# State-space layers of a hybrid network on one core: a new order of the work on TensorE, VectorE, ScalarE and GpSimd, and z in another PSUM bank

## The reference, cut to what matters

```
for i in range(6):
    residual = hidden if residual is None else hidden + residual
    h = rmsnorm(residual, norm_w[i])
    u, z = split(h @ in_w)                      # 64 -> 2 x 128
    uc = silu(causal_conv4(u) + cb)
    dt_r, Bm, Cm = split(uc @ xp_w)             # 16, 16, 16
    dt = softplus(dt_r @ dt_w + dt_b)
    # per channel d and state s, over the 256 positions:
    #   state = exp(dt * A) * state + dt * uc * Bm ;  y = sum_s state * Cm
    y = scan(uc, dt, -exp(A_log), Bm, Cm) + uc * D
    hidden = (y * silu(z)) @ out_w
```

## Time and profile before

| | us |
|---|---|
| median of 3 timed runs (lowest, highest) | 526.92 (526.82, 527.38) |
| the profiled execution | 528.41 |
| its span in the trace | 526.6 |
| TensorE busy (weight loads) | 376.8, 72% (255.9, 49%) |
| VectorE busy | 335.8, 64% |
| ScalarE busy | 256.5, 49% |
| GpSimd busy | 220.5, 42% |
| mean granted clock of TensorE | 0.826 of 2.4 GHz |

### The profile page before, as it was taken

One profiled execution on the slowest core, in us unless ns is written; L12 is line 12 of the kernel. 1 busy time (PEld: TensorE's weight loads), 2 busy tenths in 40 slices (PEclk: granted clock), 3 DMA queues, 4 the chain that ended last, 5 costly groups with the idle time before them and its releaser, 6 DMA issues.

```text
span 526.6 us, 5516 instructions
## 1 busy us (share of the span) xinstructions
PE 376.8 (72%) x1634; PEld 255.9 (49%) x1634; DVE 335.8 (64%) x577; ACT 256.5 (49%) x679; POOL 220.5 (42%) x218
## 2 busy tenths in 40 slices
PE   5753799769995894557878568587856878786563
PEld 3542566446664532235556345455644555564442
DVE  3984665445553432277777877777777777778773
ACT  1300366436561633565556565555656555565132
POOL 0760690000000002286657667665766666577000
PEclk9975899979996796557878897977889678787967
DMA  7500000000000000324051341405134150413000
GB/s 278 224 1 1 0 2 0 1 1 1 1 1 0 0 1 0 86 76 162 1 165 60 130 135 58 161 1 164 60 128 156 37 162 1 160 34 128 0 1 11
DMA packets 10424, 34.11 MB, mean 65 GB/s; under 512 B 2272, under 2 KB 2592, under 8 KB 10272
## 3 DMA queue, kind: packets, MB, share of 16 engines
q1 hardware_dynamic: 10400, 33.83, 18.8%
HBM read 33.49 MB, written 0.33 MB: 64 GB/s over the span
## 4 chain that ended last, share of the span: by engine, by line
PE 43%; DVE 21%; ACT 11%; issue 10%; POOL 9%; DMA 5%; POOLq 0%; SPq 0%; DVEq 0%; ACTq 0%
PE PS L521 11%; POOL big L1278 5%; DMA big<-spill 3%; PE PS L356 3%; PE PS L405 3%; PE PS L413 3%; PE PS L366 3%; PE PS L344 3%; DVE dt L862 2%; PE PS L263 2%; DVE big L880 2%; PE PS L498 2%; DVE big L890 2%; ACT sg L1080 1%; PE PS L490 1%
## 5 line engine op out<-in xcount | busy, mean ns | idle before, releaser
L521 PE MATMUL PS<-big,cst 128*128 128x256 f32 x384 | 119.9, 468 | 37.6 <-DVE big L890 37.6
L880 DVE TENSOR_TENSOR_SCAN big<-PS,big 128x1024 f32<-128x1024 f32 x48 | 109.7, 2286 | 35.7 <-POOL big L1278 35.7
L1278 POOL TENSOR_TENSOR big<-dtu,big 128x1024 f32<-128x1024 f32 x48 | 113.7, 2394 | 39.7 <-DVE dtu L869 36.0
L521 PEld LDWEIGHTS PS<-big,cst 128*128 128x128 f32 x384 | 87.2, 236 | 57.1 <-DVE big L890 42.4
L1112 ACT ACTIVATE PS<-dt,amat 128x255 f32<-128x255 f32 x192 | 78.9, 459 | 19.8 <-DVE dt L866 13.0
L890 DVE TENSOR_TENSOR big<-big,PS 128x1024 f32<-128x1024 f32 x48 | 58.4, 1216 | 3.5 <-PE PS L508 3.0
L977 ACT ACTIVATE big<-PS 128x512 f32<-128x512 f32 (+1 forms) x49 | 29.1, 596 | 51.9 <-PE PS L344 28.2
L1219 POOL TENSOR_TENSOR hbias<-wmt,half_t 128x1 f32<-128x1 f32 x6 | 1.2, 194 | 124.6 <-PE PS L476 124.6
L508 PE MATMUL PS<-stack,pick_b 96*128 96x256 bf16 x192 | 34.4, 309 | 11.7 <-DVE big L890 9.6
L733 DVE TENSOR_REDUCE big<-PS 128x2 f32<-128x512 f32 x32 | 22.1, 691 | 28.0 <-PE PS L405 15.3
L1014 ACT ACTIVATE big<-PS,big 128x256 f32<-128x256 f32 x64 | 29.6, 472 | 13.0 <-DVE big L733 13.0
(11 more groups left out here) (253 smaller groups left out, 676.4 us busy)
## 6 DMA issues: line engine op xcount, KB each, us to landing
big<-spill SPq DMA_DIRECT2D x48, 512.0 KB, 5.8
wmt<-in_wm SPq DMA_DIRECT2D x6, 418.0 KB, 3.3
w3t<-in_w SPq DMA_DIRECT2D x1, 1588.0 KB, 13.1
w2t<-in_w SPq DMA_DIRECT2D x1, 896.0 KB, 9.9
cst<-in_const SPq DMA_DIRECT2D x1, 848.0 KB, 7.6
w5t<-in_w SPq DMA_DIRECT2D x1, 812.0 KB, 14.9
w0t<-in_w SPq DMA_DIRECT2D x1, 416.5 KB, 3.8
w1t<-in_w SPq DMA_DIRECT2D x1, 385.0 KB, 8.1
```

Of the source, the lines that this page charges most:

```text
L521: last = pe.matmul(yps, ident, hc[:, g, s], start=False, stop=(g == NSG - 1 and s == SG - 1), skip_group_check=True)
L880: v.tensor_tensor_scan(flat(hst[g % 2][:]), flat(da[g % 2]), flat(dbu[:, g]), 0.0, ALU.mult, ALU.add).then_inc(sem("m_h"), 1)
L1278: pool.tensor_tensor(dbu[:, g], dtu[b][:].unsqueeze(1).to_broadcast([P, SG, N]), bsp[b][:, SG * g:SG * (g + 1)], ALU.mult).then_inc(sem("m ...
```

## The change

Nothing is computed differently; the same instructions are issued in another order, with other waits, and z is written to another bank. In a step u the orders are now:
- VectorE: polynomial/dt/dtu(u), gate(u-1), residual(u-1), scan 0, C product 0, scan 1, C product 1, uc(u+1), scan 2, C product 2, scan 3, C product 3.
- TensorE: sums 3 of u-1, out projection(u-1), C spread 0, skip product, transposes(u+1), C spread 1, in-projection(u+1), sums 0, x-projection(u+1), C spread 2, dt projection(u+1), sums 1, C spread 3, sums 2.
- ScalarE: decay 0, norm, decay 1, layer weights, ht, decay 2, Tanh part, first half of decay 3, xd, second half of decay 3, softplus.
- GpSimd: product 1, scale, (layer weights), product 2, product 3, (rates), gz and stack, product 0 of u+1.

`zps` is moved to bank 7, beside `ups`. The first Tanh waits for the z matmul, and uc waits for ScalarE's copy of z (`m_zs`).

```diff
-        yps, zps = PS[:, 6, 0:N], PS[:, 6, N:2 * N]
+        yps = PS[:, 6, 0:N]
-        tr, dtp = PS[:, 7, N:2 * N], PS[:, 7, N:2 * N]
+        tr, zps, dtp = (PS[:, 7, N:2 * N] for _ in range(3))
...
-                pe.matmul(ups, wcv[k][:, P:2 * P], ht[b][:, 1:1 + N], start=False, stop=True).then_inc(sem("m_up"), 1)
-                pe.matmul(zps, WM.of(wmt[k], "inz", 64), ht[b][0:64, 3:3 + N], start=opens, stop=True,
-                          skip_group_check=True).then_inc(sem("m_zp"), 1)
+                pe.matmul(ups, wcv[k][:, P:2 * P], ht[b][:, 1:1 + N], start=False, stop=True)
+                pe.matmul(zps, WM.of(wmt[k], "inz", 64), ht[b][0:64, 3:3 + N], start=True, stop=True)\
+                    .then_inc(sem("m_zp"), 1)
...
                 pe.wait_ge(sem("m_stack"), u + 1)
-                spread_c(u, b, 0)
                 if not first:
                     out_proj(u + -1, pk, nb)
+                spread_c(u, b, 0)
                 sum_skip(u, k, b)
+                if not last:
+                    prep_transpose(u + 1, nk, nb)
                 pe.wait_ge(sem("m_hc"), u * NSG + 1)
                 spread_c(u, b, 1)
                 if not last:
-                    prep_transpose(u + 1, nk, nb)
+                    prep_in(u + 1, nk, nb, i * 2 + (s + 1) // 2 + 1)
                 sum_y(u, b, 0)
                 if not last:
-                    prep_in(u + 1, nk, nb, i * 2 + (s + 1) // 2 + 1)
+                    prep_x(u + 1, nk, nb)
                 pe.wait_ge(sem("m_hc"), u * NSG + 2)
                 spread_c(u, b, 2)
                 if not last:
-                    prep_x(u + 1, nk, nb)
+                    prep_dt(u + 1, nk, nb)
                 sum_y(u, b, 1)
-                if not last:
-                    prep_dt(u + 1, nk, nb)
...
                 v.wait_ge(sem("m_sig"), u * 2 + 1)
+                v.wait_ge(sem("m_zs"), u + 1)
...
+                prep_dt(u, b)
+                if not first:
+                    gate(u + -1, pk, nb)
+                if not first:
+                    residual(u + -1, nb)
                 for g in range(NSG):
...
-                    if g == 0 and not first:
-                        gate(u + -1, pk, nb)
-                    if g == 2 and not last:
-                        prep_uc(u + 1, nk, nb)
-                    if g == 3 and not last:
-                        prep_dt(u + 1, nb)
...
-                    if g == 0 and not first:
-                        residual(u + -1, nb)
+                    if g == 1 and not last:
+                        prep_uc(u + 1, nk, nb)
...
-                decay(u, k, b, 0, not first)
-                decay(u, k, b, 1, not first)
+                decay(u, k, b, 0, behind=not first)
...
                     prep_norm(u + 1, nk, nb, ("ln_norm", 6 * NG) if first else None)
+                decay(u, k, b, 1, behind=not first)
+                if not last:
                     prep_weights(u + 1, nk, nb)
+                    prep_ht(u + 1, nk, nb)
                 decay(u, k, b, 2)
                 if not last:
-                    prep_ht(u + 1, nk, nb)
-                decay(u, k, b, 3)
+                    prep_sig(u + 1, nk, nb)
+                decay(u, k, b, 3, range(2))
                 if not last:
-                    prep_sig(u + 1, nk, nb)
                     prep_xd(u + 1, nk, nb)
+                decay(u, k, b, 3, range(2, SG))
+                if not last:
                     prep_softplus(u + 1, nk, nb)
...
                 if not last:
+                    prep_scale(u, b)
                     if b == 0:
                         prep_weights(i, s + 1, k)
-                    prep_scale(u, b)
-                    if b == 0:
-                        prep_rates(i, s + 1, k)
                 drive(i, s, 2, first)
                 drive(i, s, 3, first)
                 if not last:
+                    if b == 0:
+                        prep_rates(i, s + 1, k)
                     prep_gz(u, b)
```

More of the change, by code:

```diff
@@ L485, in prep_transpose, with prep_in @@
                 last.then_inc(sem("m_tr"), 1)
-            def prep_in(u, k, b, layers, opens=False):
+            def prep_in(u, k, b, layers):
                 pe.wait_ge(sem("m_ht"), u * 2 + 2)
@@ L513, in sum_skip @@
             def sum_skip(u, k, b):
-                pe.matmul(yps, dmat[k][:], uc[b][:], start=True, stop=False, skip_group_check=True)
+                pe.matmul(yps, dmat[k][:], uc[b][:], start=True, stop=False)
             def sum_y(u, b, g):
@@ L521, in sum_y @@
                     last = pe.matmul(yps, ident, hc[:, g, s], start=False,
-                                     stop=(g == NSG - 1 and s == SG - 1), skip_group_check=True)
+                                     stop=(g == NSG - 1 and s == SG - 1))
                 if g == NSG - 1:
@@ L564, in _ @@
             prep_transpose(0, 0, 0)
-            prep_in(0, 0, 0, 1, opens=True)
+            prep_in(0, 0, 0, 1)
             prep_x(0, 0, 0)
@@ L890, in v_step @@
                     v.tensor_tensor(hc[:, g], hst[g % 2][:], Cv, ALU.mult).then_inc(sem("m_hc"), 1)
-                    if g == 0 and not first:
-                        residual(u + -1, nb)
+                    if g == 1 and not last:
+                        prep_uc(u + 1, nk, nb)
             prep_uc(0, 0, 0)
-            prep_dt(0, 0)
             v_step(0, 0, first=True)
@@ L1076, in prep_sig @@
             def prep_sig(u, k, b):
-                for s, (src, ready) in enumerate(((ups, "m_up"), (zps, "m_zp"))):
-                    act.wait_ge(sem(ready), u + 1)
+                act.wait_ge(sem("m_zp"), u + 1)
+                for s, src in enumerate((ups, zps)):
                     act.activation(sg[b][:, s], src, ACT.Tanh, scale=0.5, bias=hbias[k][:] if s == 0 else 0.0)\
@@ L1104, in prep_softplus, with decay @@
                 act.activation(sp_m[b][:], dtp, ACT.Relu, bias=dtb).then_inc(sem("m_q"), 1)
-            def decay(u, k, b, g, behind=True):
-                if behind:
+            def decay(u, k, b, g, states=range(SG), behind=True):
+                if behind and states[0] == 0:
                     act.wait_ge(sem("m_h"), u * NSG + g + -1)
-                for n in range(SG):
+                for n in states:
                     col = SG * g + n
                     one = act.activation(da[g % 2][:, n, 1:N], dt[b][:, 1:N], ACT.Exp, scale=amat[k][:, col:col + 1])
-                one.then_inc(sem("m_da"), 1)
+                    if n == SG - 1:
+                        one.then_inc(sem("m_da"), 1)
             def prep_weights(u, k, b):
```

## The result

The changed kernel took 539.51 us (median of 4 runs, 538.11 to 541.11), the kernel before 527.15 beside it: ratio 1.0229, 95% interval 1.0191 to 1.0267. It is 12.4 us slower. The forecast of 529.7 was 2.8 us slower than before: the right sign, but a quarter of the size, and the time lies above the range of 517 to 538. The profiled execution took 540.22 us for a span of 538.4, 11.8 us longer than before.

A forecast was written before the change was run, and what follows sets the result against it. Bound by a per-step ring of waits from residual through scale, in-projection and softplus back to residual, 23.01 us. 11 x (23.2 - 23.01) = +2.1, +1.24 - 1.26 = 0, +0.69: +2.8, median 529.7 us, range 517 to 538.

The forecast's parts named there:

- Part 1: VectorE's last C product, gate and residual moved earlier: residual ends at most 6.3 us after polynomial start, gaining 3.9 or more.
- Part 2: New ring of waits through scan, GpSimd product, scale, in-projection, z copy, uc, scans 2 and 3: 21.55 to 23.41 us a step.
- Which clock: TensorE's transposes and in-projection after its pause: mostly at 1.2 GHz, end sometimes at 2.4, so 23.2 us a step.
- the walk: One step followed from polynomial to next polynomial: 23.41 us with TensorE at low clock, 21.55 at full clock.
- rival C: C spread for scan 2 comes late behind TensorE's sums 0: 24.3 to 25.3 us a step, 542 to 553; chance 0.18.
- Part 3: z's matmul moved to u's bank: ScalarE's first tanh and uc wait; first unit 1.24 us later, bank change itself 0.
- Part 4: Ends of the state-space stage: first step 0.69 us more, last unit's scans 1.26 us less.
- B: TensorE's clock stays up or returns before the in-projection: bound 21.55 us a step, 511.5, up to 525; chance 0.25.
- the price of the order: VectorE idle ahead of uc, waiting for ScalarE's z copy: 3.6 us a step lost.

The follow-up runs named there:

- the filler: Changed kernel plus eleven 256-column TensorE matmuls a step with unread results, ten before the transposes and one before the in-projection: 514.25 us (0.9772).
- narrow filler: Changed kernel plus the same number of unread TensorE matmuls in the same places, eleven a step, but of 16 columns: 540.44 us (1.0249).

## Why the prediction was wrong

- **Part 1** held: the residual ended 4.2 us after the polynomial (at most 6.3 forecast). The scale waited for product 1 until 7.68 all the same, as part 2 had it. Taking gate and residual back behind scan 0 cost 2.5 us a step, a lower clock included.
- **Part 2**, the new ring, held within 0.17 us at each handover up to uc. It ran at its low values.
- **"Which clock" is the step that failed.** I took the in-projection to be mostly low "and its end sometimes at 2.4", and so 23.2 instead of the 23.41 of the walk; and by the same hope I gave C 0.18. The clock came back 9 us after TensorE took up work, and not at about 5, where the in-projection ends. Not taking the low value costs 0.21 us a step, and the late return made rival C's case the rule: sums 0 took 3.78 us whole, and the C product was late by 0.57 us (rival C had 0.93, with 3.78 for the sums, where the next matmul starts 3.58 after their first, and 1.4 for x-projection and spread, where they took 1.21). 23.41 + 0.57 = 23.98; the last ten steps had 23.94. (The 1.73 us for sums at the full clock are only their piece of the chain; whole they take 1.99, and no bound here hangs on it.) In all the steps took 263.9 us where 11 x 23.2 + 0.69 = 255.9 were forecast: 8.0 of the 9.0 us by which the span's forecast was short.
- **The trace of before had a warning.** There the low clock lay at other places from step to step, and for other lengths: behind the first step, six steps with 10.2 us of it took 23.1 to 23.7 us, two with 6.8 us took 22.7 and 23.3, and two with 3.4 us took 22.1 and 22.5. I carried that mixture over. In the changed kernel each step has the 10.2 us, from the fourth on at the same place. Three of the variants came to the same 23.9 us a step; why they settle there was not tested.
- **Part 3** was right: ScalarE's first Tanh, in the first unit, follows z's matmul. From the norm scale's first instruction to the polynomial the first unit took 13.28 us instead of 11.93, 1.35 more (forecast 1.24).
- **Part 4:** the tail gave 1.20 of 1.26 us. Parts of the kernel that the change does not touch differ by -1.0 us ahead of the state-space layers and +1.9 behind them between the two profiled executions; the forecast had nothing for these, and their cause is open; that is the rest, 0.9 us.
- **The rivals:** C happened, at less than its price (24.0 against 24.3 to 25.3) but in all steps, so the time lies just below its 542 to 553. B did not happen, but its bound of 21.55 us a step is what the filler gives: 21.62.
- What I called the price of the order, VectorE's wait ahead of uc, is a symptom: moved away, the time stayed.

Shown are: the cost of the low clock (wide filler, with the narrow one against mere instructions), sums 0 as what is late behind it (the chain of waits, and uc moved without effect), and that the early residual and above all the scale's place help. Not shown are which side of the filler keeps the clock, width or shorter pause, and why the step settles at 23.9 us. The z bank alone was not tried: with z in bank 6 ScalarE would read it while the sums write that bank.

## What to carry to other kernels

Before moving work earlier on TensorE, ask what it does in the gap that this leaves, and which instructions meet the low clock behind the gap: walk the step at both clocks, and put the low value on all the work of some microseconds behind the gap (here it held through 9 us of work). A wait that a profile shows in front of an engine need not be the cost; move it away, and see whether the next one grows by as much. Matmuls nobody reads can be worth it in a chain that is bound by latency: seven of them, with the norm scale ahead of a product it does not need, turned a loss of 12 us into a gain of 23.

## What was not expected of the hardware

The granted clock stayed at 0.50 for 9 us of work that began at 350.56, with in-projection and sums 0 back to back in it. With sums 0 behind the x-projection, where TensorE idled 2.1 us in between, it was low for up to 20 us at a stretch. Eleven matmuls of 256 columns a step held it at 1.00 from 230 to 470 us, where eleven of 16 columns left it at 0.78. And four kernels (the changed one, uc behind scan 2, narrow filler, last C product ahead) came to steps of one length, 23.86 to 23.92 us, with the clock low for 10.2 us of each.
